# Mixing arguments with tokens in the partitions, one tanh, turned by transposes; one up part and the down parts of the second half in another order

## The chip, the cores and the metric

The kernel runs on one core of one Trainium2 chip. The metric is the device time of one execution in microseconds (us). The five engines of the core run their own instruction lists and meet only at semaphores: TensorE (PE, and PEld for its loads of the stationary operand), VectorE (DVE), ScalarE (ACT), GpSimd (POOL) and SyncE (SP), which here only issues DMAs.

## The reference

A layer of RWKV-6 time mixing is followed by a feed-forward layer with ternary weights; each adds its input and is normalised. The input x is 4 x 2048 x 512, in fp32. What the change touches is the mixing:

```python
xx = x_prev - x
mix = jnp.tanh((x + xx * time_maa_x) @ maa_w1).reshape(b, t, 5, E_MIX)   # E_MIX = 32
mix = jnp.einsum('btfe,fec->fbtc', mix, maa_w2)
mw, mk, mv, mr, mg = mix
xw = x + xx * (time_maa_w + mw)      # likewise xk, xv, xr, xg
r = xr @ Wr.T; k = xk @ Wk.T; v = xv @ Wv.T; g = silu(xg @ Wg.T)
w = time_decay + jnp.tanh(xw @ td_w1) @ td_w2
```

Then come the recurrence over time with a state of 32 x 32 for each of 16 heads, a normalisation over each head, the product with g and Wo, the residual and a layer norm. The feed-forward layer is a product with 2048 x 512 ternary weights, Gelu, a layer norm over 2048, the product back to 512, the residual and a layer norm.

## The kernel before

Time is cut into 32 tiles of 64 steps. With 4 sequences a tile has 256 tokens: `COLS = 256` columns where channels lie in the partitions, or two groups (`PAIRS`) of 128 where tokens do. The attention of tile `it` and the feed-forward layer of tile `it - 1` run interleaved, in an order written out by hand for every engine; tiles 2 to 31 are a hardware loop, and the last feed-forward runs `alone`. Each engine's function `tile` gives its order, and calls the parts of the feed-forward between its own. These parts are: `up(p, g)`, a quarter g of the hidden layer for half p of the tokens (PE: 32 fp16 matmuls, L704, into a bank of psF; ACT: Gelu L981, four scaled copies to HHI L990, square L992; DVE: the remainder HLO L1542 and the sum L1534); `down(p, part)`, a quarter of the product back (PE, L717, 8 fp16 matmuls); `stats`, `product`, `normed` and so on.

The mixing of tile `it + 1` is prepared at the end of tile `it`. DVE makes x + xx * time_maa_x in `XF[1]` (`mixed_by_x`, L1253). PE makes the arguments (`tanh_argument`, L397 to L405): `w1a`, the first four mixings, is 4 fp32 products with W1 as the stationary operand and 256 token columns moving, so that the 4 x 32 ranks lie in the partitions; `w1b`, the fifth, is 16 small products in four column groups. An fp32 product is two instructions in the trace. ACT (`mix_high`, L787) takes the tanh of w1a to TMA, copies TMA in rounded form to TMH, and makes two copies to MT for each mixing (`high`, counted by `mt_high`); for w1b it takes four small tanh to TMB, then TMBH. POOL (`mix_low`, L1014) waits for `tm_rounded` and makes ten subtractions TMA - TMH to MT (L1024, counted by `mt_low`). PE's `mix` (L432) then multiplies MT with the ranks W2S: `mw` between the two output products `wo0` and `wo1` (L680), `mk` and `mv` at the start of the next tile. DVE turns the result of each mixing into XF * xx (L1265). For `mw` DVE adds x itself (`decay_input`, L1276); for mk, mv, mr and mg POOL adds x (L1037) and counts `xf_ready`, for which the products of the channels wait (L447, the matmuls L454). L1037 for mk is the first POOL work of a tile, after `mix_low` of the tile before.

On PE the end of a tile is: the variance (L642), `up(1,3)`, two transposes of the deviations (L649), w1a, w1b, `down(1,0)`, eight transposes of the inverse deviations (L665), `down(1,1)`, `down(1,2)`, wo0, mw, wo1. The next tile starts with mk, td1 (L466), mv, td2 (L476), `down(1,3)`, channels k (L454), the sums (L711), the transposes of tokens (L696), the rest of k, `up(0,0)`. td2 writes the PSUM bank from which DVE reads wo1 (L1491), so it waits for that. psF has two banks, and `F_BANKS` says which one each of the twelve products of a tile takes; a writer waits for the last reader of its bank.

On ACT the end of a tile is: square root (L949), four scaled copies (L952), `up(1,2)`, `up(1,3)`, tanh of w1a (L960), `mix_high`. The next tile starts with the tanh of td1 (L834) and the exponentials. DVE at the end of a tile: `mixed_by_x`, `add(1,1)`, `remainder(1,1)`, the reciprocals (L1464, L1468), `remainder(1,2)`, the scaling of the output, `remainder(1,3)`, `add(1,2)`, `add(1,3)`, and the loop L1489 to L1497.

## Time and profile before

| What | Value |
|---|---|
| time, median of 3 runs | 2955.86 us (2953.89 to 2955.86) |
| the profiled execution | 2956.85 us, its span 2955.0 us |
| PE busy | 2871.2 us, 97% |
| PEld busy | 2115.4 us, 72% |
| DVE busy | 2469.3 us, 84% |
| ACT busy | 1991.6 us, 67% |
| POOL busy | 949.4 us, 32% |
| L399, w1a, in the whole run | 65.1 us, 264 instructions |
| L402, w1b, in the whole run | 21.6 us, 1056 instructions |
| table loads of ACT | 1283 ns each: L981 62, L949 32, L844 30, L779 1, L960 1 |

The span is the time from the first to the last instruction that the profiler recorded; the profiled execution's own time is 1.85 us longer. All times of instructions in this document are us from the start of the span. A busy PE includes the tail of each matmul after its columns have gone in, so the start of the next stage tells more of what a stage costs than its busy time does.

### The profile page before, as it was taken

The page shows a single profiled execution, that of the slowest core. Times are in us where ns is not written, and L with a number is a line of the kernel's source. Part 1 is how long each engine was busy: PE and PEld are TensorE (multiplying, and loading weights), DVE is VectorE, ACT ScalarE, POOL GpSimd, SP SyncE. Part 2 cuts the span into 40 slices and gives each one's busy share as a digit, 9 for nine tenths or more (in the row PEclk, how much of TensorE's full clock was granted, in tenths as well). Part 3 has the DMA queues.
Part 4 walks back from the last instruction along what each step waited for, and adds up shares of the span by engine and source line. Part 5 has one row for each costly group of instructions (what it writes and reads, how often), then busy time and mean ns, then how long its engine had stood idle before and what let it go on. Part 6 is the DMA issues. An engine that isn't in the chain of part 4 may idle for free.

```text
span 2955.0 us, 101539 instructions
## 1 busy us (share of the span) xinstructions
PE 2871.2 (97%) x40221; PEld 2115.4 (72%) x40221; DVE 2469.3 (84%) x5308; ACT 1991.6 (67%) x4242; POOL 949.4 (32%) x788
## 2 busy tenths in 40 slices
PE   6799999999999999999999999999999999999997
PEld 4577776777776777777777777777777777777775
DVE  7788888888888888889888889888889888888887
ACT  5476666776666776666776667766667766667764
POOL 4222333323333323333323332223333233333232
PEclk8899999999999999999999999999999999999998
DMA  5000000000000000000000000000000000000000
GB/s 218 9 17 20 20 24 16 21 20 16 23 24 13 24 20 16 23 24 13 20 24 16 23 22 15 20 23 16 23 16 21 20 16 23 24 13 24 20 16 23
DMA packets 22055, 72.42 MB, mean 25 GB/s; under 512 B 2816, under 2 KB 3072, under 8 KB 20000
## 3 DMA queue, kind: packets, MB, share of 16 engines
q1 hardware_dynamic: 21664, 66.12, 6.6%
q8 instruction: 379, 6.21, 0.9%
q14 instruction: 12, 0.10, 0.0%
HBM read 49.33 MB, written 16.78 MB: 22 GB/s over the span
## 4 chain that ended last, share of the span: by engine, by line
PE 91%; DVE 4%; issue 1%; ACT 1%; DVEq 0%; POOL 0%; POOLq 0%; ACTq 0%
PE psP L454 22%; PE psF L704 16%; PE psF L717 15%; PE psP L680 7%; PE psP L498 7%; PE psW L537 4%; PE psY L580 2%; PE psY L596 2%; PE psW L520 2%; PE psX L399 2%; DVE ARENA L1265 1%; PE psP L476 1%; PE psX L432 1%; PE psX L568 1%; PE psW L559 1%
## 5 line engine op out<-in xcount | busy, mean ns | idle before, releaser
L454 PE MATMUL psP<-ARENA,WALL 128*128 128x256 f32 x3072 | 694.7, 381 | 2.7 <-ACT ARENA L844 2.7
L779 ACT ACTIVATE ARENA<-ARENA 32x512 f32<-32x512 f32 (+3 forms) x930 | 524.3, 564 | 165.6 <-DVE ARENA L1343 69.5
L454 PEld LDWEIGHTS psP<-ARENA,WALL 128*128 128x128 f32 x3072 | 575.3, 191 | 79.6 <-issue 3.5
L1542 DVE SCALAR_TENSOR_TENSOR HIDDEN<-GG,FWB,HIDDEN 128x128 f16<-128x128 f32 x1024 | 347.6, 399 | 295.2 <-ACT HIDDEN L990 294.0
L1024 POOL TENSOR_TENSOR MT<-ARENA 32x256 fp32r<-32x256 f32 x330 | 349.1, 1058 | 422.8 <-ACT ARENA L779 394.2
L704 PE MATMUL psF<-XHI,WFC 128*128 128x128 f16 x4032 | 480.8, 220 | 1.6 <-DVE ST L1565 1.6
L704 PE MATMUL psF<-XLO,WFC 128*128 128x128 f16 x4032 | 479.3, 220 | 0.0
L717 PE MATMUL psF<-WPJ,HIDDEN 128*128 128x512 f16 x2016 | 473.2, 380 | 2.0 <-ACT GG L981 2.0
L1037 POOL TENSOR_TENSOR ARENA<-ARENA,XT 128x1024 f32<-128x1024 f32 x128 | 279.5, 2184 | 493.4 <-DVE ARENA L1265 478.7
L704 PEld LDWEIGHTS psF<-XHI,WFC 128*128 128x128 f16 x4032 | 391.7, 98 | 40.2 <-issue 32.5
L704 PEld LDWEIGHTS psF<-XLO,WFC 128*128 128x128 f16 x4032 | 395.7, 98 | 17.6 <-issue 10.3
L990 ACT ACTIVATE HIDDEN<-GG,FWB 128x128 f16<-128x128 f32 x1024 | 327.3, 390 | 25.4
L1066 POOL TENSOR_TENSOR ARENA<-ARENA,CF 32x512 f32<-32x512 f32 x32 | 40.6, 1270 | 918.3 <-PE psY L596 918.3
L717 PEld LDWEIGHTS psF<-WPJ,HIDDEN 128*128 128x128 f16 x2016 | 181.7, 98 | 206.3 <-issue 2.3
L981 ACT ACTIVATE GG<-psF 128x512 f32<-128x512 f32 x252 | 149.0, 591 | 159.8 <-PE psP L454 135.9
L680 PE MATMUL psP<-WALL,ARENA 128*128 128x512 f32 x512 | 230.3, 592 | 0.0
L498 PE MATMUL psP<-WALL,ARENA 128*128 128x512 f32 x512 | 227.6, 598 | 0.0
L779 ACT ACTIVATE ARENA<-psP 128x256 f32<-128x256 f32 (+1 forms) x192 | 93.7, 527 | 162.5 <-PE psP L454 162.5
L981 ACT ACT_TABLE_LOAD x62 | 79.5, 1283 | 155.5 <-PE psP L498 153.1
L1265 DVE SCALAR_TENSOR_TENSOR ARENA<-psX,PAR,XX 128x256 f32<-128x256 f32 x324 | 141.1, 476 | 39.5 <-PE psX L432 39.4
L498 PEld LDWEIGHTS psP<-WALL,ARENA 128*128 128x128 f32 x512 | 95.9, 192 | 108.8 <-issue 108.8
L1534 DVE TENSOR_TENSOR SUMS<-SUMS,GG 128x1024 f32<-128x1024 f32 x128 | 168.4, 1315 | 1.1
(199 smaller groups left out, 5015.5 us busy)
## 6 DMA issues: line engine op xcount, KB each, us to landing
XT<-x_ch SPq DMA_DIRECT2D x33, 520.0 KB, 4.3
ARENA<-x_tok SPq DMA_DIRECT2D x32, 512.0 KB, 3.9
out<-OUTX SPq DMA_DIRECT2D x64, 256.0 KB, 2.0
WALL<-w_all SPq DMA_DIRECT2D x5, 1024.0 KB, 19.2
ARENA<-wfc SPq DMA_DIRECT2D x3, 1024.0 KB, 11.2
WPJ<-wfc SPq DMA_DIRECT2D x1, 1024.0 KB, 17.2
WPJ<-wpj SPq DMA_DIRECT2D x1, 1024.0 KB, 21.3
GG<-wpj SPq DMA_DIRECT2D x1, 1024.0 KB, 23.3
```

What stands on the lines that cost most here:

```text
L454: mm = pe.matmul(psP[:, P.bank(f"{name}{g}"), COLS * c:COLS * (c + 1)], WALL[:, w, k, 128 * (2 * g + c):128 * (2 * g + c + 1)], cc(XF[slot ...
L498: mm = pe.matmul(psP[:, P.bank(f"v{p}"), :], cc(XF[1], k)[:, 128 * p:128 * (p + 1)], WALL[:, W_V, k, :], start=(k == 0), stop=(k == KC - 1))
L680: mm = pe.matmul(psP[:, P.bank(f"wo{p}"), :], cc(YSB, k)[:, 128 * p:128 * (p + 1)], WALL[:, W_O, k, :], start=(k == 0), stop=(k == KC - 1))
L704: mm = pe.matmul(bank[:, 128 * m:128 * (m + 1)], WFC[:, k, 128 * (4 * g + m):128 * (4 * g + m + 1)], x[:, p, k, :], start=(k == 0 and part ...
L717: mm = pe.matmul(bank, h[:, m, :], WPJ[:, m, :], start=(m == 0 and h is HHI), stop=(m == MH - 1 and h is HLO))
L779: return act.activation(o, i, ACT.Copy)
L981: act.activation(GG[:, u % 2, 0, :], bank, ACT.Gelu).then_inc(f_act, 1)
L990: e = act.activation(HHI[:, k, :], GG[:, u % 2, 0, 128 * m:128 * (m + 1)], ACT.Copy, scale=FWB[:, 0, k:k + 1])
L1024: pool.tensor_tensor(MT[f][rows(1 + 2 * (n % 2)), :], whole, high, ALU.subtract).then_inc(mt_low, 1)
L1037: pool.tensor_tensor(v, v, xcur, ALU.add).then_inc(xf_ready, 1)
L1265: e = dve.scalar_tensor_tensor(out=cc(XF[(f + 1) % 2], k), in0=M_BANKS[M.bank(f"{name}{g}")][:, COLS * c:COLS * (c + 1)], scalar=PAR[:, k, ...
L1542: e = dve.scalar_tensor_tensor(out=HLO[:, k, :], in0=GG[:, u % 2, 0, 128 * m:128 * (m + 1)], scalar=FWB[:, 0, k:k + 1], in1=HHI[:, k, :], ...
```

## The change

The arguments of all five mixings are made with the tokens in the partitions: XF is the stationary operand and the 160 columns of W1 move, 8 products, all into one bank. One tanh takes 2 x 160 columns to `TANH`, which lies where RM was. PE turns the result with four transposes (two of 128 columns and two of 32) into the other bank, and ACT copies it to TMA, TMH, TMBH and TMB before it makes the ten copies to MT. POOL's `mix_low` still waits for the rounded copy TMH. In each engine's order: on PE `down(1,0)` takes the place of `up(1,3)`, `down(1,1)` follows the arguments, and `up(1,3)` and the turned tanh stand between the transposes L665 and `down(1,2)`; on ACT the tanh stands ahead of `up(1,2)` and `up(1,3)`, the copies behind them; on DVE `remainder(1,1)` goes ahead of `add(1,1)`, and both additions L1491 go ahead of both bn_stats. F_BANKS is changed so that `fc3_1` and `st_1` take bank 1 and `pj_1` bank 0. Setup makes the arguments in the same new way.

```diff
-F_BANKS = [0, 1, 0, 1, 0, 1, 1, 0, 1, 0, 1, 0]
+F_BANKS = [0, 1, 0, 1, 0, 1, 1, 0, 1, 1, 0, 1]
...
+        TANH = RM[:, 0:PAIRS * 5 * MIXR].rearrange("p (q e) -> p q e", q=PAIRS)
...
-            def tanh_argument(name):
...
+            def tanh_arguments():
+
+                ps = M_BANKS[M.bank("w1a")]
+                for p in range(PAIRS):
+                    for k in range(KC):
+                        mm = pe.matmul(ps[:, 5 * MIXR * p:5 * MIXR * (p + 1)], cc(XF[1], k)[:, 128 * p:128 * (p + 1)], W1[:, k, :],
+                                       start=(k == 0), stop=(k == KC - 1))
+                return mm
+
+            def turned_tanh():
+
+                ps = M_BANKS[M.bank("w1b")]
+                for p in range(PAIRS):
+                    pe.transpose(ps[:, 128 * p:128 * (p + 1)], TANH[:, p, 0:4 * MIXR], IDENT)
+                for p in range(PAIRS):
+                    mm = pe.transpose(ps[0:MIXR, COLS + 128 * p:COLS + 128 * (p + 1)], TANH[:, p, 4 * MIXR:5 * MIXR], IDENT)
                 return mm
...
                 if ffn:
-                    ffn.up(1, 3)
+                    ffn.down(1, 0)
                 pe.wait_ge(deviations, it + 1)
...
-                for name in ("w1a", "w1b"):
-                    wait_free(name)
-                    tanh_argument(name).then_inc(m_full, 1)
-                if ffn:
-                    ffn.down(1, 0)
+                wait_free("w1a")
+                tanh_arguments().then_inc(m_full, 1)
+                if ffn:
+                    ffn.down(1, 1)
...
                 if ffn:
-                    ffn.down(1, 1)
+                    ffn.up(1, 3)
+                pe.wait_ge(tm_ready, M.read(it, "w1a"))
+                wait_free("w1b")
+                turned_tanh().then_inc(m_full, 1)
+                if ffn:
                     ffn.down(1, 2)
...
-            def mix_high(t, arguments, n):
-
-                act.wait_ge(tm_ready, M.read(t, "w1a"))
-                copy(TMH.bitcast(F32R), TMA[:, :]).then_inc(tm_rounded, 1)
-                high(t, 0)
-                act.wait_ge(arguments, n)
+            def mix_high(t, turned, n):
+
+                act.wait_ge(turned, n)
                 ps = M_BANKS[M.bank("w1b")]
-                for q in range(4):
-                    e = act.activation(TMB[:, CH * q:CH * (q + 1)], ps[MIXR * q:MIXR * (q + 1), 0:CH], ACT.Tanh)
-                e.then_inc(tm_ready, 1)
-                for f in range(1, 4):
+                copy(TMA, ps[:, 0:COLS])
+                copy(TMH.bitcast(F32R), ps[:, 0:COLS]).then_inc(tm_rounded, 1)
+                copy(TMBH.bitcast(F32R), ps[0:MIXR, COLS:2 * COLS]).then_inc(tm_rounded, 1)
+                copy(TMB, ps[0:MIXR, COLS:2 * COLS]).then_inc(tm_ready, 1)
+                act.wait_ge(tm_ready, M.read(t, "w1b"))
+                for f in range(5):
                     high(t, f)
-                act.wait_ge(tm_ready, M.read(t, "w1b"))
-                copy(TMBH.bitcast(F32R), TMB[:, :]).then_inc(tm_rounded, 1)
-                high(t, 4)
...
                 e.then_inc(y_affine, 1)
+                act.wait_ge(m_full, M.full(it, "w1a"))
+                act.activation(TANH, M_BANKS[M.bank("w1a")][:, 0:PAIRS * 5 * MIXR].rearrange("p (q e) -> p q e", q=PAIRS),
+                               ACT.Tanh).then_inc(tm_ready, 1)
                 if ffn:
                     ffn.up(1, 2)
                     ffn.up(1, 3)
-
-                act.wait_ge(m_full, M.full(it, "w1a"))
                 act.wait_ge(mt_low, 10 * (it + 1))
-                act.activation(TMA[:, :], M_BANKS[M.bank("w1a")][:, 0:COLS], ACT.Tanh).then_inc(tm_ready, 1)
                 mix_high(it, m_full, M.full(it, "w1b"))
...
                 if ffn:
+                    ffn.remainder(1, 1)
                     ffn.add(1, 1)
-                    ffn.remainder(1, 1)
...
                         mix(it + 1, 1, "mk", None)
+                for p in range(PAIRS):
                     dve.wait_ge(p_dve, P.read(it, f"wo{p}"))
                     dve.bn_stats(BNS[:, p, :], X1[:, p, :]).then_inc(bn_done, 1)
```

## Rows read from the trace of the kernel before

**Rows 1.** The page, part 1: busy time, share of the span, instructions.
```profile
PE 2871.2 (97%) x40221; PEld 2115.4 (72%) x40221; DVE 2469.3 (84%) x5308; ACT 1991.6 (67%) x4242; POOL 949.4 (32%) x788
```

**Rows 2.** Waits: engine, tile, line, waited for: us in total, times, longest.
```profile
PE psP L476 <- DVE OUTX L1491: 20.6, 30, 0.7
```

**Rows 3.** Lines by form, PE: shapes, count | busy us, mean ns | idle before.
```profile
L665 PE MATMUL psP<-CF,ARENA 128*128 128x128 f32 x256 | 33.9, 276 | 2.1 <-DVE ARENA L1468 2.1
```

**Rows 4.** Timeline of PE, one tile's end: start, us, engine, line, count, idle before.
```profile
1543.64 0.64 PE L642 MATMUL psP<-ARENA,CF 128*32 128x256 f32 x8
...
1546.00 0.39 PE L649 MATMUL psP<-CF,ARENA 128*128 128x128 f32 x2
1546.23 1.90 PE L399 MATMUL psX<-ARENA,W 128*128 128x256 f32 x8
1548.06 0.65 PE L402 MATMUL psY<-ARENA,W 128*32 128x64 f32 x32
1548.64 1.90 PE L717 MATMUL psF<-WPJ,HIDDEN 128*128 128x512 f16 x8
1550.38 1.04 PE L665 MATMUL psP<-CF,ARENA 128*128 128x128 f32 x8
...
1554.71 3.60 PE L680 MATMUL psP<-WALL,ARENA 128*128 128x512 f32 x8
1557.74 0.80 PE L432 MATMUL psX<-MT,W2S 128*128 128x256 f32 x2
...
1565.39 1.16 PE L476 MATMUL psP<-TZ,TD 64*128 64x128 f32 x16 [0.68 <-DVE OUTX L1491]
...
1568.22 3.62 PE L454 MATMUL psP<-ARENA,WALL 128*128 128x256 f32 x16
```

**Rows 5.** Timeline of ACT, one gate and the same tile's end.
```profile
1512.39 0.57 ACT L892 ACTIVATE ARENA<-psP 128x512 f32<-128x512 f32 x1
...
1546.45 1.28 ACT L981 ACT_TABLE_LOAD   x1
...
1550.16 0.57 ACT L981 ACTIVATE GG<-psF 128x512 f32<-128x512 f32 x1
...
1552.55 0.36 ACT L960 ACTIVATE ARENA<-psX 128x256 f32<-128x256 f32 x1
1552.94 0.42 ACT L779 ACTIVATE ARENA<-ARENA 128x256 fp32r<-128x256 f32 x1
```

**Rows 6.** Timeline of POOL; the second row is one subtraction inside the run of ten.
```profile
1553.44 1.70 POOL L1024 TENSOR_TENSOR MT<-ARENA 32x256 fp32r<-32x256 f32 x2 [12.27 <-ACT ARENA L779]
...
1556.21 1.79 POOL L1024 TENSOR_TENSOR MT<-ARENA 32x256 fp32r<-32x256 f32 x1
...
1563.26 1.52 POOL L1024 TENSOR_TENSOR MT<-ARENA 32x256 fp32r<-32x256 f32 x2 [0.16 <-POOL MT L1024]
1565.27 2.18 POOL L1037 TENSOR_TENSOR ARENA<-ARENA,XT 128x1024 f32<-128x1024 f32 x1 [0.49 <-POOL MT L1024]
```

**Rows 7.** Timeline of DVE, the same tile's end.
```profile
1549.77 1.14 DVE L1542 SCALAR_TENSOR_TENSOR HIDDEN<-GG,FWB,HIDDEN 128x128 f16<-128x128 f32 x4 [0.58 <-ACT HIDDEN L990]
...
1556.20 2.88 DVE L1534 TENSOR_TENSOR SUMS<-SUMS,GG 128x1024 f32<-128x1024 f32 x2
...
1561.29 1.23 DVE L1276 TENSOR_TENSOR ARENA<-ARENA,XT 128x1024 f32<-128x1024 f32 x1
...
1564.06 0.68 DVE L1497 BATCH_NORM_STATS2 BNS<-OUTX 128x6 f32<-128x512 f32 x1
1564.66 0.68 DVE L1491 TENSOR_TENSOR OUTX<-psP,ARENA 128x512 f32<-128x512 f32 x1
```

**Rows 8.** Timelines of DVE and PE around the next tile's first up part.
```profile
1575.44 0.75 DVE L1586 SCALAR_TENSOR_TENSOR OUTX<-psF,FSC,OUTX 128x512 f32<-128x512 f32 x1
...
1576.40 0.22 PE L704 MATMUL psF<-XHI,WFC 128*128 128x128 f16 x1
```

**Rows 9.** Windows near the end: stretch, us, busy by engine, PE clock, DMA.
```profile
2912.30:2917.10 4.80, 4.80 (x47) 4.80 (x47) 3.62 (x10) 1.24 (x4) 1.09 (x2) 0.50 0.02 3
```

More of the change, by code:

```diff
@@ L392, in spread_sums @@
                 mm.then_inc(su_pe, 1)
-            def tanh_argument(name):
-                ps = M_BANKS[M.bank(name)]
-                for k in range(KC):
-                    if name == "w1a":
-                        mm = pe.matmul(ps[:, 0:COLS], W1[:, k, 0:4 * MIXR], cc(XF[1], k), start=(k == 0), stop=(k == KC - 1))
-                    else:
-                        for q in range(4):
-                            mm = pe.matmul(ps[MIXR * q:MIXR * (q + 1), 0:CH], W1[:, k, 4 * MIXR:5 * MIXR],
-                                           cc(XF[1], k)[:, CH * q:CH * (q + 1)], start=(k == 0), stop=(k == KC - 1),
-                                           skip_group_check=True)
+            def tanh_arguments():
[11 more added lines that the diff above has]
+                    mm = pe.transpose(ps[0:MIXR, COLS + 128 * p:COLS + 128 * (p + 1)], TANH[:, p, 4 * MIXR:5 * MIXR], IDENT)
                 return mm
@@ L414, in _ @@
             pe.wait_ge(xm_ready, 1)
-            tanh_argument("w1a").then_inc(tm_first, 1)
-            tanh_argument("w1b").then_inc(tm_first, 1)
+            tanh_arguments().then_inc(tm_first, 1)
+            pe.wait_ge(tm_ready, 1)
+            turned_tanh().then_inc(tm_first, 1)
             def ranks_split(groups):
@@ L785, in high @@
                 copy(MT[f][rows(2), :], src).then_inc(mt_high, 1)
-            def mix_high(t, arguments, n):
-                act.wait_ge(tm_ready, M.read(t, "w1a"))
-                copy(TMH.bitcast(F32R), TMA[:, :]).then_inc(tm_rounded, 1)
-                high(t, 0)
-                act.wait_ge(arguments, n)
-                ps = M_BANKS[M.bank("w1b")]
-                for q in range(4):
-                    e = act.activation(TMB[:, CH * q:CH * (q + 1)], ps[MIXR * q:MIXR * (q + 1), 0:CH], ACT.Tanh)
-                e.then_inc(tm_ready, 1)
-                for f in range(1, 4):
+            def mix_high(t, turned, n):
+                act.wait_ge(turned, n)
+                ps = M_BANKS[M.bank("w1b")]
+                copy(TMA, ps[:, 0:COLS])
[4 more added lines that the diff above has]
+                for f in range(5):
                     high(t, f)
-                act.wait_ge(tm_ready, M.read(t, "w1b"))
-                copy(TMBH.bitcast(F32R), TMB[:, :]).then_inc(tm_rounded, 1)
-                high(t, 4)
             act.wait_ge(ranks_in, 16 * 2)
@@ L807, in _ @@
             act.wait_ge(tm_first, 1)
-            act.activation(TMA[:, :], psX[:, 0:COLS], ACT.Tanh).then_inc(tm_ready, 1)
+            act.activation(TANH, psX[:, 0:PAIRS * 5 * MIXR].rearrange("p (q e) -> p q e", q=PAIRS), ACT.Tanh).then_inc(tm_ready, 1)
             mix_high(-1, tm_first, 2)
@@ L1021, in mix_low @@
                         pool.wait_ge(tm_rounded, 2 * t + 4)
+                        pool.wait_ge(tm_ready, M.read(t, "w1b"))
                     f = n // 2
```

## The prediction

> **What bounds the kernel now.** I read the busy shares first: TensorE is busy for 2871.2 us, 97% of the span [rows 1], so in the loop over tiles nearly all time is its own work, and a change can gain only in the few places where it waits. The list of waits names one that comes back in every tile: the matmuls of `td2` (L476) wait for DVE's addition L1491, 20.6 us in 30 times [rows 2]. Then I read one tile's end on each engine in order of time: on PE from the variance matmul L642 to the first channel matmul of the next tile [rows 4], on ACT [rows 5], on POOL [rows 6], on DVE [rows 7]. There the reader should see a second chain that is nearly as late as TensorE and doesn't show in the busy shares. ACT makes the tanh (L960) and its rounded copy, POOL starts its ten subtractions (L1024) at 1553.44, ends them at 1563.26 + 1.52 = 1564.78, and only then adds x to the mixed keys (L1037, 1565.27 to 1567.45), which the channel matmuls `k` wait for. They start at 1568.22: the chain has 0.77 us to spare. All depends on whether the change moves that chain by more.
>
> **TensorE's own work.** Removed are w1a's 8 and w1b's 32 instructions, 1546.23 to 1548.64: 2.41 us [rows 4]. Added are 8 fp32 products of 160 columns, 16 instructions. L399 runs 256 columns at (1548.06 - 1546.23) / 8 = 0.229 us each [rows 4], 0.894 ns a column, so 160 columns take 0.143 us and all 16 take 2.3 us. The load of a 128x128 fp32 operand for each might be a floor. The nearest row is L665, which loads one for each 128 columns and takes 33.9 / 256 = 0.13 us an instruction [rows 3], so the columns should rule; I take 2.3 and keep 2.2 to 2.7. The four transposes are of L665's kind: 0.5 us, and 0.1 for one more change of operand (bounds 0.4 to 0.9). Together TensorE gets about +0.5 us a tile. The parts `down(1,0)`, `down(1,1)` and `up(1,3)` are only permuted: a down part is 1550.38 - 1548.64 = 1.74 us wherever it stands, and their inputs are in time. `down(1,0)` and `(1,1)` need HLO; the remainder (1,1) now goes ahead of the addition for that reason.
>
> **DVE.** The second L1491 now goes ahead of the first bn_stats (L1497), which started 0.60 us before it [rows 7]. That takes about 0.6 of the 0.68 us [rows 4] off the wait for L476 and costs nothing, since the statistics wait for both anyway. Taken alone: -0.6 + 0.5, minus what of the 0.5 falls into the part of the wait that is left, hence -0.3 a tile. If nothing else moved, this would be the change.
>
> **ACT.** The sum of its work hardly changes: one tanh of 320 columns for one of 256 and four small ones, two more copies. Its order does. The new tanh stands ahead of `up(1,2)` and needs the arguments from PE. On PE they now follow the variance (1543.64 + 0.5) and `down(1,0)` (1.74), the turning (0.23) and 2.3 us of their own: 1548.4. ACT had its Gelu of (1,2) at 1546.45 + 1.28 = 1547.73; now it waits, and Gelu (1,2) comes at about 1549.1. The table load L981 of 1546.45 moves ahead of the new tanh and lies in this wait. No load is added: gate's tanh L892 at 1512.39 runs straight after Gelu work, and the next Gelu after it has none [rows 5]. The Trainium skill ("ScalarE: Activation LUTs", table sets) lists tanh with exp and with sigmoid but not with gelu; by that list a load would come between the new tanh and Gelu, and this is a rival below. The row speaks against it.
>
> **The step that decides.** `up(1,3)` on PE moves from before 1546.00 to just ahead of the turned tanh. In the old order the third down part ended where L680 started, 1554.71; in the new order the same stages stand ahead of the last down part, so `up(1,3)` ends at 1554.71 - 1.74 - 0.1 = 1552.85. Its last matmul (0.22 long, L704 in [rows 8]) and the semaphore take 0.3, so Gelu (1,3) starts at 1553.15 where it was 1550.16 [rows 5]. Gelu, four scaled copies and the square take ACT 1552.55 - 1550.16 = 2.39: 1555.54. Now come TMA (about 0.41, as TMH's 0.42 [rows 5]) and TMH: 1556.35. POOL starts at about 1556.4, 3.0 us later than before. The turned tanh on PE (1553.4) is not what is late, ACT's `up(1,3)` is.
>
> **POOL's ten subtractions.** Undisturbed, two take 1.52, so one per 0.80. One that falls on DVE's L1534 took 1.79 in place of 0.72 [rows 6]. DVE's remainder (1,3) must wait for ACT's copies. For (1,2) it started at 1549.77, 2.0 after the Gelu, and took 1.14 [rows 7]; for (1,3) that gives 1555.15 and 1556.3, so the two L1534 start where they did, at 1556.20 for 2.88 us [rows 7]. Before, subtractions 4 and 5 fell on them; now the first two do. The first ends at 1558.0 and the second at 1559.65; the other eight take 6.4, and one falls on L1276 (+1.0): 1567.05. Then 0.49 and 2.18 as before [rows 6]: 1569.75. The channel matmuls `k` start at 1569.8 in place of 1568.22: about **+1.55 us a tile**. Bounds: one collision fewer gives +0.7; the upper ends of PE's two costs and half a collision more give +2.4.
>
> PE's own way to the same place is shorter, so it adds nothing. The product `mw` waits for the second subtraction (PE is ready at 1558.5, gets it at 1559.7), all behind it on PE (wo1, `mk`, `td1`) is 1.2 later, DVE's four L1265 and L1491 end near 1566.3, L476 starts at 1566.3 in place of 1565.39, and `k` would start at 1569.1. So the gain from DVE's reordering is gone: its place is taken by the waits for `mw`, and for `k`.
>
> One more wait is new: with F_BANKS changed, the next tile's first up part uses the bank of the product (1,·), so it waits for L1586, which ends at 1575.44 + 0.75 = 1576.19, and L704 starts at 1576.40 [rows 8]. Both follow TensorE's own stages, so they move together; 0.2 is spare. I cost it at nothing (0.3 a tile if it is missed).
>
> **The sum.** 30 boundaries of full tiles x 1.55 = 46.5. The setup, the first tile and the last have the same chain with idle engines: the extra TMA copy, the transposes and the later POOL, about 1.5 each: 4.5. Sum +51. The profiled execution took 2956.85 (span 2955.0), so 3007.9; it is 1.0 over the median of the runs, so 3007.
>
> **Rivals.** (a) The chain fits and TensorE stays the bound. If the subtractions missed the two L1534 (2 x 0.85) or POOL started before 1554.6, L1037 would end under 1568.0, `mw` would come in time, and the -0.3 would stand: -9 + 4.5, hence 2951. The turn from gain to loss is at L1037's end near 1568.0. For it: the collisions, which one row of POOL shows to cost more than the operation, are the largest term. Against: both L1534 and POOL's start hang on the same ACT instructions of (1,3), 1.4 apart, so they meet in every tile. Chance 14%, of it 8% faster, the rest within. (b) A table load of 1.28 as L981's comes between tanh and Gelu: Gelu (1,2) 1.3 later, the remainder (1,2) and z_ready 1.3 later, L1534 later and onto one more subtraction: +0.6 a tile, 3026. 5%. (c) The granted clock falls. At the end of the run, after TensorE waits of several us, it was 0.50 for 4.8 us (1.2 of 2.4 GHz) [rows 9]; half of these 4.8 us a tile would be +72: 3079. New waits of 1.2, about 0.5 and 0.6 us stand 4 us or more apart, with full work between. 3%. By the Trainium skill ("TensorE: Matmul & The Clock Gate", PE-mode transpose) transposes don't count as work for the clock, which speaks for (c); here the eight of L665 run in every tile at full clock. (d) The cost of the delay is hidden elsewhere and nothing moves: 4%.
>
> **How the numbers follow.** Forecast, +0.7 to +2.4 a tile with 2 to 8 us around it: 2979 to 3036, chance 74%; (b) lies inside, so the range holds 79%. About 0.2% is what a measurement can tell from no change: faster 8%, same 10%, slower 82%.
>
> **What would show it.** In the profile after: L1024 begins some 3 us later against L642; POOL no longer waits before L1037; PE waits for L1024 before L432 and for L1037 before L454, in 30 tiles; the wait for L1491 is under 0.2; 126 table loads as before; TensorE busy up by about 16 us and its idle time by 30. Wrong if L1037 ends within 0.8 us of where it did against L642, or if PE's wait is named L1586.

## The result: 2.8% slower, the predicted sign and a larger size

| | before | after |
|---|---|---|
| median of the runs, us | 2955.16 (2953.89 to 2955.86) | 3038.78 (3030.57 to 3045.16) |
| profiled execution, us | 2956.85 | 3030.57 |
| its span, us | 2955.0 | 3028.8 |
| TensorE busy / not busy, us | 2871.2 / 83.8 | 2902.0 / 126.8 |
| mean granted TensorE clock | 0.990 | 0.992 |

The ratio is 1.0282, with a 95% interval of 1.0257 to 1.0307: slower by 83.6 us in the medians. The forecast was 3007, with 2979 to 3036. The time is 32 us above the forecast and 3 above the range. Both profiled executions can be compared as they are, and there the difference is 73.8 us of span. The other 10 us are of another kind: the kernel after spreads over 15 us from run to run where the one before spreads over 2, and its profiled run is its quickest.

**The page after.** Part 1 of the page (engine, busy us, share, instructions), to be read against [rows 1]:

```profile
PE 2902.0 (96%) x39561; PEld 2133.9 (70%) x39561; DVE 2478.6 (82%) x5308; ACT 2029.0 (67%) x4207; POOL 941.6 (31%) x788
```

TensorE has 660 matmuls fewer (a tile has 16 products where 40 stood, and four transposes are new), yet is busy 31 us longer; its time without work is up by 43 us. The lines of the change by form, PE (line, shapes, count | busy us, mean ns | idle before), first of the kernel before and then of the one after:

```profile
L399 PE MATMUL psX<-ARENA,W 128*128 128x256 f32 x264 | 65.1, 390 | 3.2 <-DVE ARENA L1253 3.2
L402 PE MATMUL psY<-ARENA,W 128*32 128x64 f32 x1056 | 21.6, 222 | 0.0
```

```profile
L400 PE MATMUL psX<-W,ARENA 128*128 128x160 f32 x528 | 83.9, 314 | 4.7 <-DVE ARENA L1260 4.7
L408 PE MATMUL psY<-CF,ARENA 128*128 128x128 f32 x66 | 12.8, 276 | 0.5 <-ACT ARENA L814 0.5
L410 PE MATMUL psY<-CF,ARENA 128*32 128x128 f32 x66 | 12.6, 273 | 0.0
```

They come to 109.3 for 86.7: 22.6 of the 31.

**The waits after** (engine, tile, line, waited for: us in total, times, longest), to be read against [rows 2]:

```profile
PE psP L473 <- DVE ARENA L1283: 24.9, 31, 0.8
PE psP L690 <- DVE ARENA L1485: 23.5, 32, 0.7
PE psY L603 <- issue: 10.6, 22, 1.0
PEld psP L483 <- DVE OUTX L1498: 9.0, 30, 0.3
```

The wait of `td2` for the second addition (L1491 before, L1498 now) is gone, but for 0.3 us of its operand load. Two waits for DVE that the prediction didn't have are in its place, 0.7 and 0.8 us a tile: ahead of the first output product `wo0` (L690, waiting for z) and of `td1` (L473, for the decay's input). The third is of another sort: TensorE stands still before L603, far from any line of the change, and nothing releases it ("issue").

**Where a tile's time went.** I cut each tile in two at marks that both kernels have. Segment A is the tile's end, from the variance matmul (L642 before, L649 after) to the next tile's first channel matmul (L454, L461): all that the change touches lies in it, but for the wait that F_BANKS can bring. Segment B is the rest. The means are over the tiles from the third on, the sums over all 31 (the first A is 30.8 and 30.9), in us. Head is the time before the first variance, tail that behind the last:

| | A | B | sum of A | sum of B | head | tail |
|---|---|---|---|---|---|---|
| before | 24.63 | 64.70 | 770.3 | 2007.4 | 105.6 | 71.7 |
| after | 26.49 | 65.43 | 825.4 | 2028.5 | 100.6 | 74.3 |

So 55.0 us come from A, 21.1 from B, and head and tail together give back 2.4: 73.7. Where 1.55 a tile was predicted, A rose by 1.86; B stood in the prediction with no change at all, and there lies the larger error. B's excess is in one place: from the first L603 to the first L631 (L596 and L624 before) a tile takes 8.53 us on average where it took 7.95, 18 of the 21 us.

**Segment A on PE**, timeline of one tile (start, us, engine, line, count, idle before it in brackets), answering [rows 4]:

```profile
1573.89 0.64 PE L649 MATMUL psP<-ARENA,CF 128*32 128x256 f32 x8
...
1576.41 2.42 PE L400 MATMUL psX<-W,ARENA 128*128 128x160 f32 x16
1578.67 1.89 PE L727 MATMUL psF<-WPJ,HIDDEN 128*128 128x512 f16 x8
...
1586.48 3.70 PE L690 MATMUL psP<-WALL,ARENA 128*128 128x512 f32 x8 [0.75 <-DVE ARENA L1485]
1589.62 0.79 PE L439 MATMUL psX<-MT,W2S 128*128 128x256 f32 x2
...
1595.37 1.09 PE L473 MATMUL psP<-ARENA,TD 128*64 128x128 f32 x16 [0.81 <-DVE ARENA L1283]
...
1600.37 3.72 PE L461 MATMUL psP<-ARENA,WALL 128*128 128x256 f32 x16
```

The channel matmuls start 26.48 after the variance, 24.58 in [rows 4]. L439, the product that was forecast to wait 1.2 for POOL, follows L690's first matmuls without a gap: L690 itself came late.

**ACT in the same tile**, timeline, answering [rows 5]:

```profile
1576.73 1.28 ACT L961 ACT_TABLE_LOAD   x1
1578.87 0.44 ACT L961 ACTIVATE ARENA<-psX 128x320 f32<-128x320 f32 x1 [0.85 <-PE psX L400]
1579.32 1.28 ACT L987 ACT_TABLE_LOAD   x1
1580.62 0.60 ACT L987 ACTIVATE GG<-psF 128x512 f32<-128x512 f32 x1
...
1585.68 1.15 ACT L789 ACTIVATE ARENA<-psY 128x256 f32<-128x256 f32 x4
```

There are two table loads, one ahead of the tanh and one behind it. Over the kernel the loads are 157 in place of 126: lines by form, ACT, the two groups of this place and their neighbour.

```profile
L987 ACT ACT_TABLE_LOAD x62 | 79.5, 1283 | 154.6 <-PE psP L505 153.1 <-PE psF L714 1.0
L961 ACT ACT_TABLE_LOAD x32 | 41.1, 1283 | 0.6
```

Gelu(1,2) comes 6.73 us after the variance (1580.62), where 5.5 was forecast (1549.1 - 1543.64). All behind it on DVE is later.

**POOL and DVE in the same tile**, timelines, answering [rows 6] and [rows 7]:

```profile
1586.39 1.68 POOL L1031 TENSOR_TENSOR MT<-ARENA 32x256 fp32r<-32x256 f32 x2 [14.94 <-ACT ARENA L789]
1588.24 7.58 POOL L1031 TENSOR_TENSOR MT<-ARENA 32x256 fp32r<-32x256 f32 x6 [0.17 <-POOL MT L1031]
...
1598.07 2.18 POOL L1044 TENSOR_TENSOR ARENA<-ARENA,XT 128x1024 f32<-128x1024 f32 x1 [0.49 <-POOL MT L1031]
```

```profile
1586.35 2.13 DVE L1550 SCALAR_TENSOR_TENSOR HIDDEN<-GG,FWB,HIDDEN 128x128 f16<-128x128 f32 x4
1588.40 3.41 DVE L1542 TENSOR_TENSOR SUMS<-SUMS,GG 128x1024 f32<-128x1024 f32 x2
...
1594.02 1.22 DVE L1283 TENSOR_TENSOR ARENA<-ARENA,XT 128x1024 f32<-128x1024 f32 x1
```

POOL starts 12.50 after the variance (9.80 in [rows 6] against [rows 4]) and ends L1044 at 1600.25, 0.12 before the channel matmuls. DVE is later by more than its start: the remainder (1,3) takes 2.13 beside the first subtractions, where it takes 1.14 without them, and the two L1542 take 3.41 in place of 2.88 beside the six of 7.58 (1.26 each). In the kernel before they ran beside such subtractions too, and took 2.88, so why they are longer here stays open. Two chains, POOL's and DVE's by way of `td1`, arrive within a few tenths of each other; which of them sets A only an experiment tells.

### The profile page after: what moved, and what is told of

It reads as the page before. It is cut to its first block, busy times and chain, and to the rows that moved or that the text cites. A ratio compares the mean times of both kernels' runs of the same rounds, so it can differ in the third digit from the quotient of the medians.

```text
span 3028.8 us, 100216 instructions
## 1 busy us (share of the span) xinstructions
PE 2902.0 (96%) x39561; PEld 2133.9 (70%) x39561; DVE 2478.6 (82%) x5308; ACT 2029.0 (67%) x4207; POOL 941.6 (31%) x788
## 3 DMA queue, kind: packets, MB, share of 16 engines
q8 instruction: 378, 6.19, 0.8%
## 4 chain that ended last, share of the span: by engine, by line
PE 75%; DVE 12%; issue 5%; ACT 4%; DVEq 0%; ACTq 0%; POOL 0%; POOLq 0%
PE psP L461 22%; PE psF L714 13%; PE psF L727 11%; PE psP L505 7%; PE psW L544 4%; DVE ARENA L1272 3%; DVE HIDDEN L1550 3%; PE psY L603 2%; PE psX L400 2%; PE psY L587 2%; PE psW L527 2%; DVE SUMS L1542 2%; ACT HIDDEN L996 1%; DVE ARENA L1483 1%; DVE OUTX L1498 1%
## 5 line engine op out<-in xcount | busy, mean ns | idle before, releaser
L461 PE MATMUL psP<-ARENA,WALL 128*128 128x256 f32 x3072 | 696.2, 381 | 2.7 <-ACT ARENA L850 2.7
L1550 DVE SCALAR_TENSOR_TENSOR HIDDEN<-GG,FWB,HIDDEN 128x128 f16<-128x128 f32 x1024 | 332.5, 385 | 377.7 <-ACT HIDDEN L996 376.4
L461 PEld LDWEIGHTS psP<-ARENA,WALL 128*128 128x128 f32 x3072 | 571.9, 190 | 86.8 <-issue 12.0
L789 ACT ACTIVATE ARENA<-ARENA 32x512 f32<-32x512 f32 (+1 forms) x864 | 497.0, 575 | 170.6 <-DVE ARENA L1350 67.3
L1031 POOL TENSOR_TENSOR MT<-ARENA 32x256 fp32r<-32x256 f32 x330 | 338.6, 1026 | 514.9 <-ACT ARENA L789 484.5
L714 PE MATMUL psF<-XHI,WFC 128*128 128x128 f16 x4032 | 479.6, 220 | 4.2 <-DVE OUTX L1594 3.9
L727 PE MATMUL psF<-WPJ,HIDDEN 128*128 128x512 f16 x2016 | 478.5, 380 | 5.2 <-DVE HIDDEN L1550 4.8
L714 PE MATMUL psF<-XLO,WFC 128*128 128x128 f16 x4032 | 478.3, 219 | 0.0
L1044 POOL TENSOR_TENSOR ARENA<-ARENA,XT 128x1024 f32<-128x1024 f32 x128 | 279.7, 2186 | 469.6 <-DVE ARENA L1272 454.9
L714 PEld LDWEIGHTS psF<-XHI,WFC 128*128 128x128 f16 x4032 | 391.4, 98 | 35.0 <-issue 25.2
L714 PEld LDWEIGHTS psF<-XLO,WFC 128*128 128x128 f16 x4032 | 395.1, 98 | 15.9 <-issue 10.3
L727 PEld LDWEIGHTS psF<-WPJ,HIDDEN 128*128 128x128 f16 x2016 | 179.2, 98 | 221.5 <-DVE HIDDEN L1550 13.6
L690 PE MATMUL psP<-WALL,ARENA 128*128 128x512 f32 x512 | 233.6, 599 | 23.5 <-DVE ARENA L1485 23.5
L1542 DVE TENSOR_TENSOR SUMS<-SUMS,GG 128x1024 f32<-128x1024 f32 x128 | 185.0, 1446 | 1.1
L690 PEld LDWEIGHTS psP<-WALL,ARENA 128*128 128x128 f32 x512 | 92.2, 189 | 131.6 <-issue 92.3
L987 ACT ACT_TABLE_LOAD x62 | 79.5, 1283 | 154.6 <-PE psP L505 153.1
L505 PEld LDWEIGHTS psP<-WALL,ARENA 128*128 128x128 f32 x512 | 96.0, 192 | 108.9 <-issue 108.9
```

The costliest lines, as they stand in the source:

```text
L461: mm = pe.matmul(psP[:, P.bank(f"{name}{g}"), COLS * c:COLS * (c + 1)], WALL[:, w, k, 128 * (2 * g + c):128 * (2 * g + c + 1)], cc(XF[slot ...
L505: mm = pe.matmul(psP[:, P.bank(f"v{p}"), :], cc(XF[1], k)[:, 128 * p:128 * (p + 1)], WALL[:, W_V, k, :], start=(k == 0), stop=(k == KC - 1))
L690: mm = pe.matmul(psP[:, P.bank(f"wo{p}"), :], cc(YSB, k)[:, 128 * p:128 * (p + 1)], WALL[:, W_O, k, :], start=(k == 0), stop=(k == KC - 1))
L714: mm = pe.matmul(bank[:, 128 * m:128 * (m + 1)], WFC[:, k, 128 * (4 * g + m):128 * (4 * g + m + 1)], x[:, p, k, :], start=(k == 0 and part ...
L727: mm = pe.matmul(bank, h[:, m, :], WPJ[:, m, :], start=(m == 0 and h is HHI), stop=(m == MH - 1 and h is HLO))
L789: return act.activation(o, i, ACT.Copy)
```

## The experiments

All times are medians of the runs, each against runs of the kernel before on the same chip. Edits are against the kernel after unless it says otherwise. A and B are the two segments, from each run's profile.

**1. Gelu's tables first.** One Gelu of a single element, whose result nobody reads, ahead of the new tanh:

```diff
                 e.then_inc(y_affine, 1)
+                act.activation(PAUSE[:, 7:8], ZERO[0:1, :], ACT.Gelu)
                 act.wait_ge(m_full, M.full(it, "w1a"))
```

> The changed kernel with a one-element Gelu ahead of ACT's tanh of the arguments, so that the table load between tanh and Gelu (1.28 us) is gone: one load of Gelu's set serves both. Segments of a tile in the changed kernel's profile: from the variance matmul to the first channel matmul 26.49 us (before: 24.6), the rest 65.4 on average (before 64.7). Theory 1, two chains tie (POOL's subtractions start only after ACT's part (1,3), and DVE's chain that the table load made late): Gelu (1,2) comes 1.3 us earlier, but POOL starts at the same 12.5 us after the variance, the first segment stays at 26.2 to 26.5 and the time within 10 us of the changed kernel's. Rival, the table load alone makes the tile long: the first segment falls to about 25.2, the time by about 40 us.

**2. POOL's way early.** The turned tanh on PE goes ahead of `up(1,3)`, and ACT makes Gelu(1,3) behind the tanh's copies:

```diff
-                if ffn:
-                    ffn.up(1, 3)
                 pe.wait_ge(tm_ready, M.read(it, "w1a"))
                 wait_free("w1b")
                 turned_tanh().then_inc(m_full, 1)
                 if ffn:
+                    ffn.up(1, 3)
                     ffn.down(1, 2)
...
                 copy(TMB, ps[0:MIXR, COLS:2 * COLS]).then_inc(tm_ready, 1)
+                if between:
+                    between()
...
                 if ffn:
                     ffn.up(1, 2)
-                    ffn.up(1, 3)
                 act.wait_ge(mt_low, 10 * (it + 1))
-                mix_high(it, m_full, M.full(it, "w1b"))
+                mix_high(it, m_full, M.full(it, "w1b"), (lambda: ffn.up(1, 3)) if ffn else None)
```

> The changed kernel with PE's turned tanh ahead of up(1,3), and ACT's four copies of it ahead of its up(1,3) too, so POOL starts 2.4 us earlier (10.1 after the variance, before the change 9.8). The table load stays. Theory 1, two chains tie: the first segment stays at 26.2 to 26.5, as DVE's chain (z_ready, the sums, decay_input, td1) still ends there; time within 10 us of the changed kernel's. Rival, POOL's late start alone, as my prediction had it: the first segment falls to 25, the time by about 45 us.

**3. Both edits.**

> Both edits at once: the one-element Gelu ahead of the tanh, and the turned tanh with its copies ahead of up(1,3). Theory 1, two chains tie: only now the first segment falls, to 24.9 to 25.3, and the time by 35 to 50 us against the changed kernel's (about 2990). If one of the two chains alone binds, this run equals the better of the two single edits.

Measured:

| | ratio to before [95%] | median | A | POOL starts after the variance | B |
|---|---|---|---|---|---|
| after | 1.0282 [1.0257, 1.0307] | 3038.8 | 26.49 | 12.50 | 65.43 |
| 1 Gelu first | 1.0259 [1.0242, 1.0276] | 3032.1 | 26.24 | 12.49 | 65.60 |
| 2 POOL early | 1.0326 [1.0309, 1.0343] | 3050.6 | 26.96 | 9.85 | 65.39 |
| 3 both | 1.0212 [1.0195, 1.0229] | 3018.7 | 25.79 | 8.76 | 65.54 |

ACT in experiment 1, timeline of one tile (variance at 1579.17):

```profile
1581.99 1.28 ACT L960 ACT_TABLE_LOAD   x1
1583.28 0.20 ACT L960 ACTIVATE PAUSE<-CF 1x1 f32<-1x1 f32 x1
1584.15 0.44 ACT L962 ACTIVATE ARENA<-psX 128x320 f32<-128x320 f32 x1 [0.67 <-PE psX L400]
1584.49 0.59 ACT L988 ACTIVATE GG<-psF 128x512 f32<-128x512 f32 x1
```

The load now comes for the small Gelu, the tanh of 320 columns runs on the same tables, and Gelu(1,2) follows with no load 5.32 after the variance, near the 5.5 of the prediction. With that the tile is what the prediction had drawn. PE and POOL of the same tile, timelines:

```profile
1595.14 0.50 PE L439 MATMUL psX<-MT,W2S 128*128 128x256 f32 x2 [1.03 <-POOL MT L1032]
...
1605.40 0.91 PE L461 MATMUL psP<-ARENA,WALL 128*128 128x256 f32 x3 [0.46 <-ACT ARENA L850]
```

```profile
1591.66 3.42 POOL L1032 TENSOR_TENSOR MT<-ARENA 32x256 fp32r<-32x256 f32 x2 [14.96 <-ACT ARENA L789]
...
1603.10 2.17 POOL L1045 TENSOR_TENSOR ARENA<-ARENA,XT 128x1024 f32<-128x1024 f32 x1 [0.49 <-POOL MT L1032]
```

The first two subtractions fall on DVE's L1543 and take 3.42 together, the product L439 waits 1.03 for them (1.2 forecast), and the channel matmuls start 0.13 after L1045 ends at 1605.27. The wait of 0.46 before them is put down to ACT L850, but L1045 ended last, so it is POOL's. Yet A falls by only 0.25: the table load is worth little while POOL's chain stays as late. The time, 3032.1, is 7 us lower and inside the forecast range.

In experiment 2 it is the other way round. Timelines of PE and POOL (variance at 1588.69):

```profile
1610.72 1.09 PE L473 MATMUL psP<-ARENA,TD 128*64 128x128 f32 x16 [0.83 <-DVE ARENA L1283]
```

```profile
1598.54 1.96 POOL L1031 TENSOR_TENSOR MT<-ARENA 32x256 fp32r<-32x256 f32 x2 [12.31 <-ACT ARENA L788]
...
1612.24 2.17 POOL L1044 TENSOR_TENSOR ARENA<-ARENA,XT 128x1024 f32<-128x1024 f32 x1 [2.74 <-DVE ARENA L1272]
```

POOL starts 2.65 earlier, and then waits 2.74 us for a DVE that is later than ever, since Gelu(1,3) is later. A rises by 0.47, where it was expected to stay. Both edits together bring A down by 0.70, where their single effects add up to +0.22: each frees one of two chains that end together. In the kernel after, then, neither the late POOL nor the table load alone is "the" cause of A's size; each covers for the other. I had expected more of the two, 24.9 to 25.3 for A and about 2990 us. In experiment 3 Gelu(1,3), 9.8 after the variance in place of 6.5 in [rows 5], brings DVE's remainder (1,3) onto the subtractions (2.67 us where it takes 1.14), and `td1` still waits 0.84 for DVE.

**4. The new arithmetic in the old order.** The products with tokens in the partitions, the one tanh and the transposes stay, and so does DVE's reordering. PE's parts, ACT's order and F_BANKS go back:

```diff
-F_BANKS = [0, 1, 0, 1, 0, 1, 1, 0, 1, 1, 0, 1]
+F_BANKS = [0, 1, 0, 1, 0, 1, 1, 0, 1, 0, 1, 0]
...
-                    ffn.down(1, 0)
+                    ffn.up(1, 3)
                 pe.wait_ge(deviations, it + 1)
...
                 tanh_arguments().then_inc(m_full, 1)
                 if ffn:
-                    ffn.down(1, 1)
+                    ffn.down(1, 0)
...
                 if ffn:
-                    ffn.up(1, 3)
+                    ffn.down(1, 1)
                 pe.wait_ge(tm_ready, M.read(it, "w1a"))
...
-                act.wait_ge(m_full, M.full(it, "w1a"))
-                act.activation(TANH, M_BANKS[M.bank("w1a")][:, 0:PAIRS * 5 * MIXR].rearrange("p (q e) -> p q e", q=PAIRS),
-                               ACT.Tanh).then_inc(tm_ready, 1)
                 if ffn:
                     ffn.up(1, 2)
                     ffn.up(1, 3)
+                act.wait_ge(m_full, M.full(it, "w1a"))
+                act.activation(TANH, M_BANKS[M.bank("w1a")][:, 0:PAIRS * 5 * MIXR].rearrange("p (q e) -> p q e", q=PAIRS),
+                               ACT.Tanh).then_inc(tm_ready, 1)
```

> The new arguments, the one tanh and the transposes, but in the old order on PE and ACT (up(1,3) after the variance, down(1,0) after the arguments, down(1,1) and the turned tanh after the transposes of the inverse deviations, ACT's tanh behind up(1,3), the old F_BANKS); DVE's new order stays. No table load is added, POOL starts about 1.1 us later than before the change. Theory: the order, not the arithmetic, costs most: the first segment is 24.9 to 25.2 (TensorE's own +0.5 us shows here), the time 2965 to 2990. Rival, the new form of the arguments is what costs: the time stays over 3010.

Measured 2994.7, ratio 1.0132 [1.0115, 1.0149], A 25.18, B 65.59. A is where it was expected, and so 1.31 of A's 1.86 belong to the order of PE and ACT (with the table load that it brings) and 0.55 are left for the rest, DVE's two reorderings included; the time is above what was expected, by B. Waits of PE and ACT and POOL's timeline in this kernel (variance at 1562.44):

```profile
PE psY L603 <- issue: 14.4, 25, 1.2
PE psF L727 <- ACT GG L987: 14.4, 32, 1.8
ACT GG L987 <- DVE SUMS L1539: 20.2, 32, 2.8
```

```profile
1573.74 3.58 POOL L1031 TENSOR_TENSOR MT<-ARENA 32x256 fp32r<-32x256 f32 x2 [13.75 <-ACT ARENA L789]
...
1585.32 2.18 POOL L1044 TENSOR_TENSOR ARENA<-ARENA,XT 128x1024 f32<-128x1024 f32 x1 [0.49 <-POOL MT L1031]
```

Even so POOL starts 1.5 later than before. Not all of that is the tanh's new way by ACT, PE and ACT again. Gelu(1,2) waits here in every tile for DVE's `add(1,1)` (L1539), which before was in time (5.4 us in 2 waits): it is the other reordering on DVE, `remainder(1,1)` ahead of `add(1,1)`, that makes it late. Both Gelus start 0.5 later against the variance than before (1569.46 - 1562.44 = 7.02 for (1,3), 6.52 before), and PE's next down part waits 0.4 a tile for the first. L1044 ends 25.06 after the variance, and the channel matmuls follow at 25.18.

**5. The two additions ahead of both bn_stats, alone**, in the kernel before (`remainder(1,1)` stays behind `add(1,1)`):

```diff
                         mix(it + 1, 1, "mk", None)
+                for p in range(PAIRS):
                     dve.wait_ge(p_dve, P.read(it, f"wo{p}"))
                     dve.bn_stats(BNS[:, p, :], X1[:, p, :]).then_inc(bn_done, 1)
```

> The kernel before with DVE's part alone: both additions L1491 ahead of both bn_stats. Theory (the prediction's term): the wait of L476, 0.68 us in 30 tiles, falls under 0.15, nothing else moves, first segment 24.0 to 24.1, second 64.7: 2955 - 0.55 x 30 = 2938. Rival: another wait ends as late (mk's result, the exponentials on ACT) and the time stays within 4 us.

Measured 2936.8 (2936.3 to 2941.0), ratio 0.9939 [0.9926, 0.9953]: 19 us faster than the kernel before, and the fastest of all versions run here. A is 24.04 (-0.59), B 64.73. A row of the waits and one of PE's timeline:

```profile
PEld psP L476 <- DVE OUTX L1491: 9.0, 30, 0.3
```

```profile
1553.02 1.16 PE L476 MATMUL psP<-TZ,TD 64*128 64x128 f32 x16
```

What is left of the wait of [rows 2] is 0.3 of the operand's load, and the matmuls have no gap before them. The part of the change that looked smallest holds all of its gain. From here the kernel of experiment 4 costs 25.18 - 24.04 = 1.14 in A, and the new order with its table load a further 1.31. The 1.14 is not the arithmetic's alone: the Gelus that are 0.5 late for `add(1,1)` are in it. No run has the new arithmetic without that reordering, so the arithmetic's own share, some 0.6 by that difference, is an estimate.

**6. The same work, its code moved.** B is work that the change doesn't touch, and the gap in it has no releaser; it came back before L603 in experiments 1 to 4 (14.1, 12.0, 13.6 and 14.4 us). It could be a matter of where TensorE's code lies in memory: the kernel after has 20 matmuls and 20 loads a tile fewer, so every later instruction stands elsewhere. To test that without changing any work, TensorE repeats a wait that is already met in its setup. N is 128, 64 and 192 in the kernel after (6a, 6b, 6c), 128 and 64 in the kernel of experiment 4 (6d, 6e), and 128 in that of experiment 5 (6f).

```diff
-            pe.wait_ge(const_in, 16 * 4)
+            for _ in range(N):
+                pe.wait_ge(const_in, 16 * 4)
             pe.wait_ge(su_dve, 1)
```

6a, 

> The changed kernel with 128 copies of one wait that is already met at the head of PE's setup: no other work, but PE's code behind them lies 128 instructions later. In the changed kernel the second segment of a tile (first channel matmul to the next variance) is 65.43 us on average with a spread from 64.7 to 66.7, before 64.70 with almost none; the extra is PE idle before L603 with no releaser. Theory F: PE waits for its instructions there, and this depends on where the loop's code lies against the 256-instruction pieces in which it is fetched (the change shortened PE's code ahead of the loop by about 117 instructions, so 128 more nearly restore it): the second segment returns to 64.7 to 64.9, the time falls by about 20 us. Rival, a wait for data or a slower neighbour: the segment stays at 65.2 to 65.7 and the time within 6 us.

6b, 

> The changed kernel with 64 met waits in PE's setup. With none, PE's idle time without a releaser lies at L603 (10.6 us in 22 times) and the second segment of a tile is 65.43 us; with 128 it lay at L632 (the matmuls of values, 6.4 us in 17) and the segment was 65.17. Theory F (PE runs out of fetched instructions at a place that goes by the code's position): with 64 the place is a third one or the stall is gone; the first segment stays 26.49, since two data chains set it; the second is anything from 64.7 to 66. Rival (what moved it in the run with 128 was chance): the idle time is at L603 or L632 (shifted lines) again, with the second segment at 65.2 to 65.5.

6c, 

> The changed kernel with 192 met waits in PE's setup. Theory F: a fourth place or none, first segment 26.49, unless the place falls at the start of the tile (td1), where the run with the old order and 128 waits lost 2 us a tile; with 64, 128 and 192 the lowest time shows what the change costs without it: 2955 + 31 x 1.9 - 3 = 3011. Rival: as in the run with 64.

6d, 

> The new arithmetic in the old order (2994.7 us) with the same 128 met waits in PE's setup. Theory F: its second segment falls from 65.59 to about 64.8, the time to 2965 to 2975; what is then left over the kernel with DVE's part alone is TensorE's own +0.5 us and POOL's later start. Rival: no change.

6e, 

> The new arithmetic in the old order with 64 met waits. With none it took 2994.7 us with a second segment of 65.59 and PE idle at L603; with 128 it took 3044.9, as PE stood 2 us at the start of most tiles with no releaser or one long done. Theory F: the time differs from both, between 2968 (no such stall: first segment 25.18, second 64.7) and 3050, and the data chains (POOL's start 11.3 us after the variance) stay. Rival: the time is that of one of the two within 4 us.

6f, 

> The kernel before with DVE's part alone and the 128 met waits, so that old arithmetic stands at about the code position of the changed kernel (128 against 117 instructions, modulo 256). Theory F: the second segment rises from 64.7 to 65.2 to 65.7, with the spread that the changed kernel has, and the time is 15 to 30 us over that without the waits. Rival, the fetch has nothing to do with the position: the time is within 5 us of it.

| kernel, N | median | ratio [95%] | A | B | TensorE's gaps without a releaser |
|---|---|---|---|---|---|
| after, 0 | 3038.8 | 1.0282 [1.0257, 1.0307] | 26.49 | 65.43 | L603 10.6 in 22 |
| after, 64 | 3020.3 | 1.0223 [1.0206, 1.0240] | 26.49 | 64.89 | L576 3.5 in 3 |
| after, 128 | 3030.3 | 1.0247 [1.0232, 1.0263] | 26.49 | 65.17 | L632 6.4 in 17 |
| after, 192 | 3025.3 | 1.0245 [1.0228, 1.0262] | 26.50 | 64.83 | L632 0.3 in 2 |
| old order, 0 | 2994.7 | 1.0132 [1.0115, 1.0149] | 25.18 | 65.59 | L603 14.4 in 25 |
| old order, 64 | 2992.4 | 1.0132 [1.0115, 1.0149] | 25.70 | 64.89 | L474 23.3 in 29, L576 5.9 in 5 |
| old order, 128 | 3044.9 | 1.0307 [1.0292, 1.0323] | 26.85 | 65.27 | L474 26.3 in 14, L632 12.8 in 25 |
| DVE alone, 0 | 2936.8 | 0.9939 [0.9926, 0.9953] | 24.04 | 64.73 | |
| DVE alone, 128 | 2944.0 | 0.9959 [0.9944, 0.9975] | 24.00 | 64.93 | |

The rows of the waits, one fence each for 6a, 6b, 6c, 6d and 6e:

```profile
PE psY L632 <- issue: 6.4, 17, 0.6
```

```profile
PE psX L576 <- issue: 3.5, 3, 1.3
PE psP L416 <- issue: 7.5, 1, 7.5
```

```profile
PE psP L416 <- issue: 14.5, 1, 14.5
```

```profile
PE psP L474 <- DVE OUTX L1499: 33.1, 15, 2.5
PE psP L474 <- issue: 26.3, 14, 2.0
PE psY L632 <- issue: 12.8, 25, 0.9
```

```profile
PE psP L474 <- issue: 23.3, 29, 1.3
```

In the kernel after, 64 or 192 instructions that do nothing take B from 65.43 to 64.89 and 64.83, within 0.2 of before's 64.70, in spite of what they cost themselves once at the start (the 7.5 and 14.5 before L416). A stays at 26.49 to 26.50 in all four positions. The gap before L603 vanishes in each, and with 128 another comes before L632. So A's 55 us are of the change's order and arithmetic, and B's excess is of the position. The sizes were not foreseen: 128 was to bring B to 64.7 to 64.9 here (65.17 came), and in the kernel of experiment 5 it was to cost 15 to 30 us (7 came).

With the old order the same 128 do harm, 50 us, which I had not expected: the gap now falls on `td1` inside A. Timelines of PE and DVE in 6d:

```profile
1237.71 1.09 PE L474 MATMUL psP<-ARENA,TD 128*64 128x128 f32 x16 [2.33 <-DVE OUTX L1499]
```

```profile
1231.04 0.69 DVE L1499 TENSOR_TENSOR OUTX<-psP,ARENA 128x512 f32<-128x512 f32 x1 [1.43 <-PE psP L691]
...
1233.33 1.24 DVE L1284 TENSOR_TENSOR ARENA<-ARENA,XT 128x1024 f32<-128x1024 f32 x1
```

The wait of 2.33 us carries the name of DVE's L1499, but that ended at 1231.73, and the decay's input that `td1` reads (L1284) at 1234.57, 3.1 us before L474 started. Neither held it up; with the "issue" rows this is one stall under two labels. That a position costs the old order 1.7 us a tile in A (26.85 for 25.18) is shown.

What TensorE waits for there is in the trace too. Among the DMA packets are some of the kind "instruction", in the kernel after 378 on queue 8 with 6.19 MB, 16 KiB each. DMA in 6d, from 1234.8 to 1236.2 (queue, kind: packets, MB, share of 16 engines):

```profile
q8 instruction: 1, 0.02, 5.9%
```

This packet lands at 1236.15, and L474 starts 1.56 later. It is the rule: past the first tile, 24 of 24 of TensorE's gaps without a releaser in the kernel after and 39 of 39 in 6d end 1.2 to 1.85 us after such a landing, and so do 239 of 241 in all kernels of this document, though these stretches cover only 8% of the time. L474's long waits in 6d, 14 under "issue" and 15 under L1499, all do, 1.4 to 1.7 after a landing. It is the landing that counts: where the packet took 0.96 us, L474 started 2.58 after the packet did, and where it took 1.29, 2.85. So the stalls are waits for instructions, as far as times can show it; the packets don't say for which engine they are. The kernel of experiment 5 is little touched (7 us for 128; its stage from L597 to L625 takes 8.18 in place of 7.95, with no gap listed), and the kernel before was run at one position only. Why a fetch comes late at some places, and which positions are good, stays open.

## Why the prediction was right in sign and short in size

Two steps failed: the sum priced everything outside the tile's end at nothing (segment B, 21.1 us), and "No load is added" (0.25 us a tile). Undoing either alone brings the time back into the range (3020 to 3030 at other positions, 3032 in experiment 1).

- **Which chain decides** was half right. With the table load out of the way (experiment 1) the tile is the one that was drawn: Gelu(1,2) at 5.32 after the variance (5.5), wait before the product 1.03 (1.2), channel matmuls behind POOL's addition. In the kernel after POOL starts 12.50 after the variance (12.8), its addition ends 26.36 after it (26.1), and the channel matmuls start at 26.48 (26.16). But there DVE's chain ends with it, and the waits for POOL that were to be seen before the product and the channel matmuls in 30 tiles are seen only in experiment 1. The rival that the chain fits (2951) is refuted.
- **"No load is added"** failed. The row of [rows 5] was real: gate's tanh runs straight after Gelu work. It showed that the tables loaded for Gelu can serve tanh, and I took it to say that the tables loaded for tanh serve Gelu. After the square root the next instruction in need of tables is now the tanh; what is loaded for it doesn't serve Gelu, and a second load follows in each tile. The rule that I set against the row, the table sets of "ScalarE: Activation LUTs" in the Trainium skill, gave the load rightly for this place. Neither rule nor row was enough alone: by the list gate's tanh too would need a load, which the 62 loads for Gelu show it doesn't. This was rival (b), which I gave 5%. Its mechanism came true in the main: z and the sums late, waits of 0.75 and 0.8 on PE, L1542 beside later subtractions. Its price of 0.6 did not: taking the load away brings 0.25, since POOL's chain ends together with DVE's.
- **A's sum**: 1.86 a tile for 1.55, 55.0 us for 46.5. The load's 0.25 is the bulk of the difference. Some luck is in it: POOL started 0.3 earlier than forecast, and its ten subtractions took 11.19 in place of 10.65.
- **Segment B** stood at nothing in the sum, without a word. It is the larger failure: 21.1 us in the profiled run, where TensorE stands still before L603, by the landings for want of instructions. The spread from 3030 to 3045 probably belongs to it, since at the positions 64 and 192 the same kernel spreads over 4 and 3 us. An edit that takes 20 matmuls and their loads out of a tile moves all of TensorE's code, and the rows of before have no such stall that comes back, from which a bound could have come. With the code at another place (6b) the time is 3020.3, inside the range and 13 over the forecast.
- **TensorE's own work**: the 16 instructions take 2.26 us to the next one's start (2.3), and by the groups of lines the change's own work rose by 22.6 us, 0.7 a tile, for 0.5 forecast (its bounds give 0.2 to 1.2). Busy time as a whole rose by 31 for 16, idle time by 43 for 30. What is left of the 31 lies in stages that the change didn't touch but that now stand next to a gap (L727, L603, L690: 5.3, 4.8 and 3.3 more, against small falls elsewhere); why their busy time grows there I didn't test.
- **DVE's additions ahead of bn_stats** were priced exactly: 0.6 a tile, measured alone 0.59. The other reordering on DVE was priced at nothing; in the old order it costs the wait for `add(1,1)` of experiment 4. That the later chain eats the gain up was right too; the wait for the second addition in the kernel after is 0.3 of a load.
- **The wait for F_BANKS** at nothing: right. L714 waits for it once, 3.9 us, and not in the other tiles.
- **The clock** (rival c) didn't fall: 0.992 for 0.990, in spite of four transposes more and two new gaps a tile. Only 6d, with stalls of some 2 us, shows it lower: 0.985 in its slowest run. The Trainium skill's remark that a transpose is no work for the clock ("TensorE: Matmul & The Clock Gate", PE-mode transpose) took no visible effect here.
- **The head** gave back 5.1 us where a loss of about 3 stood in the sum. That is no gain of the change: with no added waits the head took 100.6 to 105.6 us in the profiled runs, and 102.9 in experiment 5, whose edit doesn't touch it. The tail took 2.6 more, for about 1.5 forecast.

## What to carry to other kernels

When an ACT function moves, ask for which function the tables were loaded last at its new place, and what the next function needs: a row with A after B free of a load says nothing of B after A. Split a mixed edit and price its parts one by one; here the reordering of two DVE additions, 0.6% faster by itself, was buried under chains that end 2.45 us a tile later (26.49 for 24.04). And where two chains end together, undoing one cause proves little (0.25 and -0.47 here, 0.70 for both); undo them singly and together.

## What the runs showed of the hardware that I had not expected

- **The same function, with and without a load.** Tanh has run on the tables of Gelu (gate, and experiment 1) and on others that don't have Gelu (after the square root), each load 1283 ns. It is what was loaded last that decides, not what comes next: a Gelu follows in both places. A single element's Gelu of 0.20 us ahead of the tanh brings the shared tables. The Trainium skill says that the compiler's back end places the loads per block, by greedy longest runs ("ScalarE activation tables: per-element evaluation and per-set limits", Table sets in the compiler and the runtime). Experiment 1 shows that one set holds both tanh and Gelu, and over the two that set would be the longer run. It wasn't taken in the kernel after (157 loads), so either a block ends between them or the rule doesn't hold here; no run tells which.
- **The place of code costs time.** With the same work, TensorE's gaps without a releaser came and went with 64 to 192 instructions that do nothing: 3020 to 3039 us for one kernel, 2992 to 3045 for another. The gaps end 1.2 to 1.85 us after a 16 KiB packet of instructions lands. At the bad positions both spread more from run to run (15 and 11 us) than the kernel before (2 to 5). Differences of 1% between kernels of unlike code length can't be given to the edit unless the stage that it touches shows them.
- **A named releaser can be innocent.** Waits of up to 2.5 us were put down to an addition that had ended 6 us before.
